# Cross attention of layer 0: exponents stay unscaled, and queries, output tiles and norms of half of the tokens stand between its pairs of heads

## What is computed

```python
hidden_states = residual + attn_out
ci = rms_norm(hidden_states, ln_post_cross_w)
cq = heads(ci @ cq_w, NH, CHD)            # 16 heads of 16
ckv = encoder_outputs @ ckv_w
ck, cv = jnp.split(ckv, 2, axis=-1)
ck, cv = (heads(ck, NH, CHD), heads(cv, NH, CHD))
cctx = sdpa(cq, ck, cv, causal=False)
cctx = cctx.transpose(0, 2, 1, 3).reshape(b, l, CC)
hidden_states = hidden_states + cctx @ cdense_w
mi = rms_norm(hidden_states, ln_post_attn_w)
v_out = jax.nn.silu(mi @ v_gate) * (mi @ v_up) @ v_down
```

## Time and profile before

| | us |
|---|---|
| median of three runs | 2068.93 |
| the three runs | 2070.44, 2068.93, 2057.18 |
| the profiled execution | 2059.55 |
| its span | 2057.7 |
| TensorE busy | 1935.4 (94%) |
| VectorE busy | 1151.7 (56%) |
| ScalarE busy | 830.2 (40%) |
| GpSimd busy | 886.8 (43%) |

### The profile page before, as it was taken

How to read it: one execution, slowest core, us unless ns; L and a number is a source line. 1 busy time by engine, 2 the same in 40 slices (tenths; PEclk the granted TensorE clock), 3 DMA queues, 4 the chain that set the end, 5 groups by cost and what they waited for, 6 DMA issues and landing times.

```text
span 2057.7 us, 35482 instructions
## 1 busy us (share of the span) xinstructions
PE 1935.4 (94%) x12588; PEld 1656.5 (80%) x12588; DVE 1151.7 (56%) x2790; ACT 830.2 (40%) x2198; POOL 886.8 (43%) x1037
## 2 busy tenths in 40 slices
PE   4999979998899999999999999998979999999998
PEld 3876767777799898988888878995458888887997
DVE  6777867776553453346767645312274666655422
ACT  2026426775221121146666613222235666652321
POOL 3340322231488999941212057860044212103885
PEclk9999988996899999999999999999989999999999
DMA  3110100001133333310000032332121000001332
GB/s 125 41 57 2 39 15 17 26 28 31 43 110 104 113 113 119 121 54 10 18 13 24 2 117 86 109 103 87 62 87 34 18 10 24 13 1 42 103 107 83
DMA packets 38189, 118.86 MB, mean 58 GB/s; under 512 B 6168, under 2 KB 10264, under 8 KB 38016
## 3 DMA queue, kind: packets, MB, share of 16 engines
q1 hardware_dynamic: 31408, 107.92, 16.8%
q10 hardware_dynamic: 6608, 8.68, 1.4%
HBM read 114.75 MB, written 1.84 MB: 57 GB/s over the span
## 4 chain that ended last, share of the span: by engine, by line
PE 80%; DVE 10%; POOL 4%; issue 2%; ACT 2%; DMA 1%; DVEq 0%; SPq 0%; ACTq 0%; POOLq 0%
PE psum L561 15%; PE psum L562 13%; PE psum L563 13%; PE psum L783 7%; PE psum L794 6%; PE psum L837 5%; PE psum L681 4%; PE psum L554 4%; PE psum L683 4%; PE psum L682 4%; POOL wl L1664 3%; DVE xc L1257 1%; DVE nmin L1348 1%; DVE rstd L1242 1%; DVE probs_t L1383 1%
## 5 line engine op out<-in xcount | busy, mean ns | idle before, releaser
L1664 POOL TENSOR_TENSOR wl<-raw,wh 128x256 fp32r<-128x256 f32 x656 | 518.6, 821 | 13.7
L561 PE MATMUL psum<-nh,wh 128*128 128x448 f32 x904 | 348.6, 386 | 14.8 <-DVEq L1440 7.9
L1656 POOL TENSOR_SCALAR wh<-raw 128x1024 fp32r<-128x1024 f32 x164 | 183.8, 1121 | 413.1 <-PE psum L563 173.8
L562 PE MATMUL psum<-nl,wh 128*128 128x448 f32 x904 | 337.0, 373 | 0.0
L563 PE MATMUL psum<-nh,wl 128*128 128x448 f32 x904 | 336.1, 372 | 0.0
L1031 ACT ACTIVATE probs_t<-masked_t,nmin 112x375 f32<-112x375 f32 (+1 forms) x384 | 202.6, 529 | 109.0 <-DVE nmin L1359 109.0
L1512 DVE TENSOR_TENSOR hid_l<-scr,hid_h 128x448 fp32r<-128x448 f32 x108 | 95.1, 881 | 228.5 <-ACT hid_h L1109 227.9
L1383 DVE TENSOR_SCALAR probs_t<-probs_t,rinv 112x376 f32<-112x376 f32 (+1 forms) x520 | 214.3, 453 | 9.4
L794 PE MATMUL psum<-cst,probs_t 112*125 112x112 f32 (+1 forms) x1304 | 198.1, 284 | 18.0 <-ACT probsT_t L1051 13.6
L794 PEld LDWEIGHTS psum<-cst,probs_t 112*125 112x125 f32 (+1 forms) x1304 | 175.0, 194 | 42.2 <-DVE probs_t L1383 24.4
L561 PEld LDWEIGHTS psum<-nh,wh 128*128 128x128 f32 x904 | 174.4, 193 | 37.8 <-issue 12.2
(11 more groups left out here) (178 smaller groups left out, 3842.1 us busy)
## 6 DMA issues: line engine op xcount, KB each, us to landing
raw<-in_walls SPq DMA_DIRECT2D x183, 512.0 KB, 3.5
raw<-in_ctxF SPq DMA_DIRECT2D x24, 375.0 KB, 3.0
ctxb<-in_ctxF ACTq DMA_DIRECT2D x8, 375.0 KB, 4.0
ctxt<-in_ctxK ACTq DMA_DIRECT2D x8, 375.0 KB
x<-in_xT ACTq DMA_DIRECT2D x2, 896.0 KB, 11.3
outT<-x SPq DMA_DIRECT2D x2, 896.0 KB, 5.8
mask<-in_kmask ACTq DMA_DIRECT2D x16, 41.0 KB, 2.6
vself<-in_tt SPq DMA_DIRECT2D x1, 448.0 KB, 6.5
```

The lines of the kernel that those rows point to most:

```text
L561: nc.tensor.matmul(out, ah, bh, start=(i == 0), stop=False)
L562: nc.tensor.matmul(out, ah, bl, start=False, stop=False)
L1656: nc.gpsimd.tensor_scalar(high, src, 1.0, 1.0, ALU.mult, ALU.mult).then_inc(split_h, 1)
L1664: last = nc.gpsimd.tensor_tensor(low[cut], src[cut], high[cut].bitcast(F32), ALU.subtract)
```

## The change

1. The exponents of this attention are no longer scaled. The transposes wait for the exponents alone. The sums of four heads get one reciprocal on VectorE, written 16 times side by side (`rexp`, in `quad_sums`); TensorE transposes that into the free half of the output's PSUM bank in each `weigh`, and the output group multiplies even and odd heads by it (`rs`). Even and odd heads are thereby picked by zeros in `rexp`.
2. Of stage "cq" only the two tiles of half 0 stand ahead of the attention. Norm 1 of half 1, cut into nine pieces, stands in turns 1 to 9, the two tiles of half 1 in turns 10 and 11.
3. Of stage "cdense" the four tiles of half 0 stand in turns 41, 42, 43 and 45, the nine pieces of norm 2 of half 0 in turns 48 to 56. The four tiles of half 1 follow the attention, and then the MLP.
4. Both norms get scratch space of their own. The weights of cdense are loaded and split behind the layout of batch 6 and ahead of the context of batch 7. The weights kv1 of layer 1 take over the scratch's place and wait for norm 2 of half 0.

The core of the diff:

```diff
-        [u for b in range(2, B) for u in ((0, "ctx0", b), (0, "mcross", b))] + uses("cdense") + with_kv1(uses("gu")) +
+        [u for b in range(2, B) for u in ((0, "ctx0", b), (0, "mcross", b)) + (tuple(uses("cdense")) if b == 6 else ())] +
+        with_kv1(uses("gu")) +
...
+        def pieces(nn, half, key):
+
+            return {key: [("norm", nn, half, p) for p in ("s0", "s1", "v", "r", "f0", "f1", "f2", "f3", "f4")]}
...
-            "cq": by_half(2, 2, parts(1, 1, s=(0, 0), v=(0, 1), f=(0, 1))),
-            "cdense": by_half(4, 4, parts(2, 0, s=(1, 0), v=(1, 1), f=(1, 1))),
+            "cq": by_half(2, 2, pieces(1, 1, (0, 1))),
+            "cdense": by_half(4, 4, pieces(2, 0, (0, 3))),
...
+        WITHIN = {1 + i: ("cq", 2 + i) for i in range(11)}
+        WITHIN.update({n: ("cdense", i) for i, n in enumerate((41, 42, 43, 45, *range(48, 57)))})
...
             def turn(a, s):
                 g = s // a.group
-                pe.wait_ge(a.scaled, s + 1)
+                pe.wait_ge(a.exped if a is att_c0 else a.scaled, s + 1)
...
+                if a is att_c0:
+                    pe.wait_ge(a.recip, u + 1)
+                    nc.tensor.transpose(pv_bank[:, (2 + u % 2) * S:(3 + u % 2) * S],
+                                        rexp[:, u % 2].rearrange("p h n -> p (h n)"), ident[0:S, 0:S])
...
+                        if a is att_c0 and n in WITHIN:
+                            name, j = WITHIN[n]
+                            (cq if name == "cq" else cdense)(items=[j])
...
-            stage("cq", nhl, KD, ("dve",), 2, nn=1)
+            cq(range(2))
             plan.use([0])
             attention(att_c0)
             pe.wait_ge(att_c0.exped, att_c0.steps)
             plan.use(range(POOL))
-
-            stage("cdense", nhl, KC, ("dve",), 4, ready=lambda half, m: pe.wait_ge(att_c0.out, att_c0.steps // 8))
+            cdense(range(13, len(SEQ["cdense"])))
...
-                    src = pick[:, :]
-                    dve.wait_ge(chain, link(nc.vector.tensor_scalar(src, pv_bank[:, 0:S], cst[:, C_EVEN:C_EVEN + 1], None,
-                                                                    ALU.mult)))
-                    dve.wait_ge(chain, link(nc.vector.scalar_tensor_tensor(src, pv_bank[:, S:2 * S], cst[:, C_ODD:C_ODD + 1],
-                                                                           src, ALU.mult, ALU.add)))
+                    even, odd = pv_bank[:, 0:S], pv_bank[:, S:2 * S]
+                    dve.wait_ge(chain, link(nc.vector.tensor_copy(rs[:, :], pv_bank[:, 2 * S:4 * S])))
+                    link(nc.vector.tensor_mul(pick[:, :], even, rs[:, 0:S]))
+                    dve.wait_ge(chain, link(nc.vector.tensor_mul(odd, odd, rs[:, S:2 * S])))
+                    src = odd
+                    dve.wait_ge(chain, link(nc.vector.tensor_add(src, src, pick[:, :])))
...
+            def quad_sums(a, u):
+
+                dve.wait_ge(a.exped, 4 * u + 4)
+                if u >= 2:
+                    dve.wait_ge(a.summed, u - 1)
+                own, j = slice(4 * (u % 2), 4 * (u % 2) + 4), u % 2
+                nc.vector.reciprocal(rexp[:, j, :, 16 * j:16 * j + 16],
+                                     rsum8[:, own].unsqueeze(2).broadcast_to([S, 4, 16])).then_inc(a.recip, 1)
...
+                    if a is att_c0:
+                        if late and n % 2 == 0:
+                            quad_sums(a, n // 2 - 1)
+                        late = ()
```

More of the change, by code:

```diff
@@ L285, in build @@
         assert 4 * NTURN * 4 * S <= place[0] - o_n
+        xc_b = at("xc_b", [P, KD, HALF], F32, o_v)
+        sq_b = at("sq_b", [P, 2, HALF], F32, o_v + 4 * KD * HALF)
+        total_b, std_b, rstd_b = [at(f"{what}_b", [P, HALF], F32, o_v + 4 * (KD + 2 + i) * HALF)
+                                  for i, what in enumerate(("total", "std", "rstd"))]
         kk2 = sb("kk2", [P, 2, 376], F32R)
@@ L590, in norm_part @@
                 kind = NORMS[nn][0]
+                total = scratch(nn, half)[2]
                 if part == "m":
@@ L952, in norm_part @@
                 kind, wname, bname, e = NORMS[nn]
+                xc, sq, _, std, _ = scratch(nn, half)
                 if part in S_PART:
@@ L983, in norm_part, with stage @@
                         ins.then_inc(nhigh, 1)
-            def stage(name, each):
-                for it in SEQ[name]:
+            def stage(name, each, items=None):
+                for j in items or range(len(SEQ[name])):
+                    it = SEQ[name][j]
                     if it[0] == "norm":
@@ L1097, in _ @@
                 context(att_1, b)
-            stage("cdense", None)
+            stage("cdense", None, range(13, len(SEQ["cdense"])))
             def hidden(name):
@@ L1206, in norm_part @@
                 w = vec[:, VECS.index(wname), :]
+                xc, sq, total, std, rstd = scratch(nn, half)
                 if part == "a":
@@ L1396, in attention @@
                         out_group(a, (w + 1) * a.pair // a.outgroup - 1)
+                    if a is att_c0 and n in WITHIN:
+                        name, j = WITHIN[n]
+                        stage(name, cq if name == "cq" else residual("cdense"), [j])
             for t in (ctxh, ctxl):
@@ L1501, in cq @@
                     .then_inc(emptied["dve"], 1)
-            stage("cq", cq)
+            stage("cq", cq, range(2))
             attention(att_c0)
-            stage("cdense", residual("cdense"))
+            stage("cdense", residual("cdense"), range(13, len(SEQ["cdense"])))
             def hidden(name, gate=None):
```

28 lines of the change are left out of this document (26 added, 2 removed).

## The result

The changed kernel takes 2055.12 us (median of 20 runs, 2050.63 to 2063.03) against 2063.03 for the kernel before (20 runs, 2057.18 to 2072.08): ratio 0.9964, 95% interval 0.9949 to 0.9979. It is 7.4 us faster, where 20 had been worked out. The time itself lies at the upper edge of the recorded forecast (2034 to 2056), but the kernel before is also faster here than in its first three runs (2068.93).

The account below looks back on a forecast made before the run. In the attention no engine alone was the bound, TensorE (90%) and VectorE (84%) trading waits; afterwards TensorE. Terms summed to -20.1 us: 2039.5 from the profiled run, 2048.8 from the median; forecast 2044, the middle (2034 to 2056, chance 0.55).

Parts of the forecast that it names:

- Start, -12.4: Before the first scores: only half 0's two query tiles stand ahead, saving 12.4 us, with TensorE still idle 4.8 us.
- End, -16.1: After the attention: half 1's 24 matmuls and the MLP's 24 follow each other, 12.0 us for 28.1, saving 16.1.
- Scaling leaves VectorE, -10.6: Inside the attention: without scalings the pace falls from 2.72 to 2.55 us a pair, 10.6 us over 64 pairs.
- Tiles and their wait, +9.7 and +2.3: Inside the attention: 48 query and output matmuls cost 9.7 us uncovered; waiting for cdense's split weights costs 2.3.
- The norms, +5.5 each, and half clock, -4: Inside the attention: each norm's pieces cost 5.5 us, 11 together; half clock falls from 16.1 us to 12.
- the upper end of 9 each: Highest cost allowed for each inside norm, 9 us: table changes, reciprocal and part of VectorE's excess added up.
- two pairs of slack: TensorE, at most two pairs of scores ahead, was taken to hide part of the norms' cost, leaving 5.5 us each.
- 64 pairs at full clock: The attention's pairs of heads at the forecast full-clock pace of 2.55 us each.
- behind the last scores: Stretch of the attention after its last scores, taken as some 10.2 us.
- the rival in which the norms give the gain back: Inside norms cost their upper 9 us, pace stays 2.65, holes bring half clock: 2063 us (2056 to 2068), chance 0.20.
- The rival of a held clock: TensorE stays at full clock but for the start, pace 2.46 us a pair: 2028 us (2022 to 2034), chance 0.17.
- the 5.5 us that were estimated from the page's drain: Four table switches on ScalarE would cost 5.5 us more by the skill page's 1.38 us drain; not in the sum.

Follow-up runs that it names:

- e1: Kernel before with only the unscaled exponents; both stages and both norms stay outside the attention: 2046.21 us, 16.1 under the kernel before.
- e4: Unscaled exponents, with only the output's tiles and norm 2 inside the attention, queries outside as before: 2051.62 us, 11.6 under the kernel before.
- e6: Changed kernel with a copy for the square root in both inside norms, so no table change there: 2054.49 us, 10.3 under the kernel before.
- e8: Changed kernel with 24 useless matmuls in TensorE's idle time ahead of the first scores: 2053.69 us, 10.3 under the kernel before.
- e10: Changed kernel with both inside norms' pieces in different turns on different engines (skewed), query tiles later: 2050.25 us, 13.2 under the kernel before.
- e5: Changed kernel with norm 1's variance piece and what follows two turns later, norm 2's squares one earlier: 2058.73 us, 5.2 under the kernel before.
- e3: Unscaled exponents, with only the queries' tiles and norm 1 inside the attention, output outside as before: 2060.24 us, 3.7 under the kernel before.
- e15: Unscaled exponents, only the queries' part inside, its pieces in different turns on different engines, tiles later: 2050.30 us, 13.4 under the kernel before.

## Why the prediction was wrong, by its steps

**Start, -12.4: right** (22.40 to 9.92). TensorE's forecast idle of 4.8 us is there, on GpSimd's layout. This row and the wait for the split weights, of which more below:

```profile
300.13 1.28 PE L806 MATMUL psum<-kk,qmx 32*112 32x376 f32 x6 [4.77 <-POOL qmx L1710]
...
434.30 0.47 PE L583 MATMUL psum<-nh,wh 128*128 128x448 f32 x1 [1.77 <-POOL wl L1734]
```

**End, -16.1: right** (28.10 to 11.93, forecast 12.0).

**Scaling leaves VectorE, -10.6: right in kind, half in size.** The full-clock pace of e1 came out at 21.05 us for eight pairs, 2.63 a pair where 2.55 was taken: 64 x (2.716 - 2.63) = 5.5 us, not 10.6. TensorE is busy for 94% of it, 2.48 us a pair, as worked out (2.46); the waits on ScalarE's copies are longer than thought. The spread reciprocal took what was forecast, 0.54 us; group of after, busy us, mean ns, idle before:

```profile
L1419 DVE RECIPROCAL rexp<-rsum 112x64 f32<-112x64 f32 x32 | 17.4, 543 | 0.0
```

e1 alone gave 16.1 us, and 14.9 in the attention (198.9 to 184.0), close to the 14.6 of this term and the -4 of half clock together. That is luck: the pace gave 5 us less than thought, and the clock, 0.90 over e1's attention where it had been 0.84, about as much more.

**Tiles and their wait, +9.7 and +2.3: near.** TensorE waits 1.77 us on GpSimd's split. Four tiles and that wait add 4.0 us to one period of four pairs (14.35 against e1's 10.38) and 2.2 to the next, 6.2 where 4.9 and 2.3 stood.

**The norms, +5.5 each, and half clock, -4: the step that failed.** Against e1 the pieces with norms are 16.9 and 21.9 us longer. Off come 4.9 us of tiles each, and 1.8 of wait: 12.0 and 15.2 us a norm, 27.2 against 11. Even the upper end of 9 each was too low. It is no accident of one execution: the eight pairs of turns 48 to 55, which hold norm 2, take 36.8 us here, 36.1 in e4, 36.4 in e6 and 37.0 in e8, against 21.0 in e1.

The pieces' rows, length less busy time, tell how it comes about. TensorE's idle time rises from 2.78 to 8.64 us and from 2.38 to 10.11; less the wait for weights that is 11.8 us for both norms, about the 11 of the forecast. The other 15.5 us are TensorE's own time: beyond the tiles it is busy for that much longer, at a clock of 0.79 and 0.84 where e1 has 0.89 and 1.00, with two matmuls more for each norm. The working put this into a term of its own and let it shrink: 12 us of half clock where there had been 16, though it named the norms as new holes. The trace has 13 us at 0.52 behind norm 2's hole, with TensorE nearly always busy:

```profile
465.00:478.00 13.00, 12.42 (x84) 9.67 (x88) 8.31 (x16) 7.51 (x16) 5.42 (x7) 0.52 0.26 85
```

The two shares aren't independent, since a TensorE at half clock hides waits that one at full clock would show. In e10, whose piece with norm 2 is at full clock throughout, the same subtraction leaves 55.49 - 42.06 - 4.9 - 1.8 = 6.7 us for what stands there of the norm, near the forecast's 5.5.

As to the holes, the working counted the table change and the reciprocal, and let two pairs of slack hide a part. It left out the first half of the norm: squares and sums stand in the same turns ahead of the attention's mins and copies, each waiting for the one before, and TensorE stands still for 4.12 and 3.68 us. e5 shows that this isn't L622's place in TensorE's queue. At norm 1 the skew takes most of the hole away (4.63 to 1.70 us) and the kernel gains 9.7 us (e3 to e15); shortening the pieces gains 15 to 19 us for both norms. Why the clock falls behind such a hole and comes back where it does, and so how the 15.5 us would divide between the pieces, stays open.

**The sum.** For the stretch of the attention in the earlier trace rows the working comes to 208.5 us, and 220.84 were measured. Term by term:

| term, us | worked out | from the traces |
|---|---|---|
| 64 pairs at full clock | 163.2 | 168.3 (2.63 a pair) |
| behind the last scores | 10.2 | 10.2 (as worked out) |
| tiles | 9.7 | 9.7 (as worked out) |
| wait for split weights | 2.3 | 1.8 |
| norms, TensorE idle | 11.0 | 11.8 |
| half clock | 12.1 | 19.0 (the rest; 7.2 in e1) |

The last row is an estimate, what is left of 220.84. So 12.3 us are missing, 7 by half clock and 5 by the pace; that is about the whole difference between the 20.1 us of the sum and the 7.4 measured. The mechanism is that of the rival in which the norms give the gain back: its conditions, the norms' upper price, a pace near 2.65 and half clock behind the holes, are what the trace shows. Its time was 2063 (2056 to 2068), and 2055.12 is just below. The rival of a held clock came true only for a part of e1.

**The table change.** On the Trainium skill's "ScalarE: Activation LUTs", "What ACT_TABLE_LOAD costs": the load took its 1.28 us; of the 1.38 us more that the page gives for a drain nothing is to be seen here. ScalarE in order of time, after:

```profile
467.41 1.28 ACT L1009 ACT_TABLE_LOAD   x1
468.70 0.63 ACT L1009 ACTIVATE std_b<-psum,eps 128x448 f32<-128x448 f32 x1
...
470.23 0.44 ACT L1099 COPY probsT_t<-psum 125x336 f32<-125x336 f32 x1 [0.57 <-PE psum L864]
470.69 1.28 ACT L1076 ACT_TABLE_LOAD   x1
471.98 0.57 ACT L1076 ACTIVATE probs_t<-psum,nmin 112x375 f32<-112x375 f32 x1
```

Root and exponents start 0.01 us behind the end of their loads, and the second load 0.02 us behind the end of the copy ahead of it. e6 puts all four switches at 2.9 us, with intervals that overlap; the 5.5 us that were estimated from the page's drain have no place in this trace.

## What to carry over

Price work that is put inside a dense stretch by what it holds up, not by its own length: follow the moved chain instruction by instruction, and ask for each what stands behind it on its engine and how far that is from the bound engine's next work. When a wait is seen in front of one instruction, move that instruction and look again: here the hole stayed (e5). Then price half clock with the holes, since it cost TensorE more than its idle time did. If it must go inside, give its steps to different turns on different engines; at the queries' norm that was worth more (9.7 us) than leaving out the table loads or the reciprocals of both (2.9 and 1.9). And time each part of a combined change alone: here one part gave 16 us and the other took half of it back.

## What the runs showed of the chip

TensorE's clock fell in stretches that were dense as well. In e1 TensorE had no gap from 392 to 401, then one of 0.77 us, and ran at half clock from about 403 to 412 while busy throughout:

```profile
398.00:400.00 2.00, 2.00 (x36) 1.56 (x36) 1.02 (x3) 1.37 (x5) 1.92 (x3) 1.00 0.03 8
400.00:402.00 2.00, 1.23 (x12) 0.82 (x11) 1.47 (x5) 1.89 (x7) 0.22 (x1) 1.00 0.39 41
402.00:404.00 2.00, 2.00 (x27) 1.72 (x30) 0.53 (x2) 1.45 (x6) 0.00 (x0) 0.56 0.54 221
404.00:406.00 2.00, 2.00 (x20) 1.21 (x13) 0.30 (x1) 0.44 (x1) 0.00 (x0) 0.50 0.00 0
```

In the changed kernel it stayed at full clock with TensorE busy for only 3.26 to 3.99 of each 5 us:

```profile
503.00:508.00 5.00, 3.99 (x51) 3.02 (x49) 3.52 (x10) 4.05 (x15) 0.00 (x0) 1.00 0.00 0
508.00:513.00 5.00, 3.26 (x45) 2.52 (x43) 3.45 (x9) 4.10 (x15) 0.00 (x0) 1.00 0.02 5
```

The same last eight turns took 22.15 us at a clock of 1.00 (e15) and 29.71 at 0.60 (e3), with the same instructions. These 7.6 us are as large as the whole effect of the change; what decides between the two was not found.
